# A new table of planned durations and a new table of priorities for the order of work on one core

## What is computed

```
x = x + 0.5 * moe0(norm(x))      # 24 experts, hidden 512, best 2 of 24 per token
x = x + linear_attention(norm(x))
x = x + 0.5 * moe0(norm(x))
x = x + 0.5 * moe1(norm(x))      # 8 experts, hidden 256, best 2 of 8, and a shared expert
x = x + causal_attention(norm(x))
x = x + 0.5 * moe1(norm(x))
```

## Time and profile before

| | us |
|---|---|
| median of 3 runs | 971.14 |
| lowest and highest | 970.65, 973.02 |
| the profiled execution's time | 970.65 |
| its span in the profile | 969.3 |

### The profile page before, as it was taken

One profiled execution on the slowest core, in us unless ns is written; L12 is line 12 of the kernel. 1 busy time (PEld: TensorE's weight loads), 2 busy tenths in 40 slices (PEclk: granted clock), 3 DMA queues, 4 the chain that ended last, 5 costly groups with the idle time before them and its releaser, 6 DMA issues. The chain is left out here.

```text
span 969.3 us, 25617 instructions
## 1 busy us (share of the span) xinstructions
PE 813.2 (84%) x9531; PEld 694.9 (72%) x9531; DVE 660.3 (68%) x2266; ACT 636.3 (66%) x1197; POOL 497.6 (51%) x519
## 2 busy tenths in 40 slices
PE   5898899998997477899999899874989998997940
PEld 3444899996886245798998789752777867786940
DVE  4798864477767897788467871479668979882122
ACT  4466788889895386688899775542748665773420
POOL 0076560065001777136366077777753575477775
PEclk9899999999999598799999999976999999998985
DMA  8789865473334323695657339842674374556852
GB/s 266 239 262 348 215 150 106 94 145 78 65 78 87 77 64 97 144 204 125 133 136 149 61 100 232 163 114 71 146 131 99 75 155 102 129 140 158 193 137 76
DMA packets 254167, 134.32 MB, mean 139 GB/s; under 512 B 171936, under 2 KB 232288, under 8 KB 254048
## 3 DMA queue, kind: packets, MB, share of 16 engines
q1 hardware_dynamic: 237664, 99.11, 44.5%
q0 software_dynamic: 16384, 33.59, 13.2%
HBM read 40.09 MB, written 56.89 MB: 100 GB/s over the span
## 5 line engine op out<-in xcount | busy, mean ns | idle before, releaser
L2540 POOL DMA_INDIRECT got<-y_l,slot_index x256 | 245.6, 960 | 249.0 <-DMA y_l<-y 83.4
L2520 POOL DMA_INDIRECT rows<-rows_sent,slot_index x192 | 189.3, 986 | 189.3 <-issue 93.9
L1711 PE MATMUL bank<-turned,first_high_l 128*128 128x128 f16 x1248 | 225.6, 221 | 23.1 <-DVE hid L2065 11.1
L1712 PE MATMUL bank<-turned,first_high_l 128*128 128x128 f16 x1248 | 225.3, 220 | 0.0
L1713 PE MATMUL bank<-turned,first_low_l 128*128 128x128 f16 x1248 | 225.2, 220 | 0.0
L2065 DVE SCALAR_TENSOR_TENSOR hid<-bank,hid 128x512 f16<-128x512 f32 x220 | 145.7, 686 | 84.2 <-ACT hid L1957 82.2
L1950 ACT ACTIVATE bank<-bank 128x512 f32<-128x512 f32 x220 | 128.4, 591 | 36.4 <-PE bank L1713 32.7
L2332 DVE SCALAR_TENSOR_TENSOR x_res<-got,share,x_res 128x128 f32<-128x128 f32 x256 | 77.6, 349 | 108.5 <-DMA got<-y_l,slot_index 106.2
L1711 PEld LDWEIGHTS bank<-turned,first_high_l 128*128 x1248 | 123.2, 99 | 30.6 <-issue 29.5
L1957 ACT ACTIVATE hid<-bank 128x512 f16<-128x512 f32 x220 | 129.0, 599 | 7.1 <-PE bank L1750 3.0
L1712 PEld LDWEIGHTS bank<-turned,first_high_l 128*128 x1248 | 123.1, 99 | 3.4 <-issue 1.9
(11 more groups left out here) (304 smaller groups left out, 1669.4 us busy)
## 6 DMA issues: line engine op xcount, KB each, us to landing
y_l<-y SPq DMA_DIRECT2D x92, 256.0 KB
rows<-own SPq DMA_DIRECT2D x14, 512.0 KB, 5.9
got<-in_w_dram SPq DMA_DIRECT2D x27, 256.0 KB, 4.5
hid<-in_w_dram SPq DMA_DIRECT2D x25, 256.0 KB, 3.6
got<-y_l,slot_index POOLq DMA_INDIRECT x256
rows<-rows_sent,slot_index POOLq DMA_INDIRECT x192, 2.4
y_l<-y SPq DMA_DIRECT2D x12, 192.0 KB
x_res<-in_x_dram SPq DMA_DIRECT2D x8, 256.0 KB, 4.5
```

The lines of the kernel that those rows point to most:

```text
L1711: t.do.matmul(out, cut_of(high[c], e), xh, start=True, stop=False)
L1712: t.do.matmul(out, cut_of(high[c], e), xl, start=False, stop=False)
L2520: d = g.do.indirect_dma_start(rows_dram[s], at, rows[:, 2 * D * i:2 * D * i + 2 * D], None)
L2540: d = g.do.indirect_dma_start(got_mem[slot][:, col:col + D], None, y_dram[layer][s][layer.team(ev.i)], at)
```

## The change

Two tables of the plan are replaced; no other line is touched. In `work`, the planned time of some steps becomes another one. The `EARLIER` table becomes another one as a whole: the entries for GpSimd (GP) and SyncE (SY) are gone, so that their steps go by 2p + s alone (unlisted expert steps on all engines but PE by -10 besides), and most entries of ScalarE (SC), TensorE (PE) and VectorE (VE) have other values.

```
-        "halve_0": [[(PE, 1.25, 0.2), (SC, 0.6, 0.1)]], "halve_1": [[(PE, 0.95, 0.2), (SC, 0.6, 0.1)]],
+        "halve_0": [[(PE, 1.1, 0.2), (SC, 0.6, 0.1)]], "halve_1": [[(PE, 0.95, 0.2), (SC, 0.6, 0.1)]],
-        "norm_a": [[(VE, 3.0, 0.1), (SC, 1.6, 0.15)]],
-        "norm_g": [[(VE, 3.0, 0.1), (SC, 1.6, 0.15)] if ev.p else [(VE, 1.15 if ev.i % 2 else 5.4, 0.1)]],
+        "norm_a": [[(VE, 2.73, 0.1), (SC, 1.6, 0.15)]],
+        "norm_g": [[(VE, 2.73, 0.1), (SC, 1.6, 0.15)] if ev.p else [(VE, 1.15 if ev.i % 2 else 5.4, 0.1)]],
-        "score": [[(PE, 0.5 if ev.p > 1 else 0.7 if ev.p else 0.95, 0.2), (VE, 0.2, 0.1)]],
-        "shared1": [[(PE, 1.6, 0.2), (SC, 1.2, 0.15)]], "shared2": [[(PE, 2.55, 0.2), (VE, 0.7, 0.1)]],
+        "score": [[(PE, 0.7 if ev.p else 0.95, 0.2), (VE, 0.2, 0.1)]],
+        "shared1": [[(PE, 1.4, 0.2), (SC, 1.3, 0.15)]], "shared2": [[(PE, 2.3, 0.2), (VE, 0.7, 0.1)]],
-        "scatter": [[(GP, 1.265 * TOP_K * tokens, 2.2)]], "gather": [[(GP, 1.23 * TOP_K * BT, 2.4)]], "add": [[(VE, 3.2, 0.1)]],
+        "scatter": [[(GP, 1.0 * TOP_K * tokens, 2.2)]], "gather": [[(GP, 1.0 * TOP_K * BT, 2.4)]], "add": [[(VE, 3.0, 0.1)]],
-        "la_qk": [[(PE, 2.3, 0.2), (SC, 1.45, 0.15)]], "la_vg": [[(PE, 1.85, 0.2), (SC, 1.3, 0.15)]],
-        "la_second": [[(PE, 2.65, 0.2), (VE, 1.4, 0.1)]], "la_soft": [[(SC, 3.7, 0.15), (VE, 1.4, 0.1)]],
-        "la_heads": [[(PE, 1.15, 0.2), (VE, 0.2, 0.1)]],
+        "la_qk": [[(PE, 1.9, 0.2), (SC, 1.3, 0.15)]], "la_vg": [[(PE, 1.85, 0.2), (SC, 1.3, 0.15)]],
+        "la_second": [[(PE, 2.8, 0.2), (VE, 1.4, 0.1)]], "la_soft": [[(SC, 3.9, 0.15), (VE, 1.4, 0.1)]],
+        "la_heads": [[(PE, 1.0, 0.2), (VE, 0.2, 0.1)]],
-        "la_out": [[(PE, 1.5, 0.2), (VE, 0.7, 0.1)]],
+        "la_out": [[(PE, 1.4, 0.2), (VE, 0.7, 0.1)]],
-        "ca_score": [[(PE, 2.4, 0.2), (VE, 3.0, 0.1), (SC, 3.3, 0.15)]], "ca_flip": [[(PE, 1.5, 0.2), (SC, 1.5, 0.15)], [(VE, 0.2, 0.1)]],
+        "ca_score": [[(PE, 2.4, 0.2), (VE, 3.0, 0.1), (SC, 3.3, 0.15)]], "ca_flip": [[(PE, 1.3, 0.2), (SC, 1.5, 0.15)], [(VE, 0.2, 0.1)]],
...
-EARLIER = {(GP, "gather"): -2, (GP, "gather", 2): -3, (GP, "scatter"): 3, (GP, "scatter", 0): 3, (GP, "scatter", 2): -4, (GP, "scatter", 3): 2,
...
- (SC, "ca_flip"): 0, (SC, "ca_score"): 3, (SC, "hid", 1): -3, (SC, "l1", 1): 0.5, (SC, "l1", 2): -1, (SC, "la_soft"): 3, (SC, "norm_a"): -3,
...
- (SY, "fetch"): -1, (SY, "fetch", 0): -4, (SY, "fetch", 1): 3, (SY, "fetch", 3): 2, (SY, "send_a"): -2, (SY, "send_g"): -1, (SY, "ystore"): -4,
...
- (PE, "ca_flip"): -4, (PE, "ca_score"): -2, (PE, "la_out"): -4, (PE, "la_second"): -2, (PE, "la_vg"): 2, (PE, "score", 2): -4,
...
- (VE, "add", 1): 0, (VE, "add", 2): 1, (VE, "add", 3): 3, (VE, "hid"): -2, (VE, "hid", 0): -3, (VE, "norm_g"): -4, (VE, "r_top"): -3, (VE, "r_norm"): -4,
...
+EARLIER = {(SC, "bias"): 0, (SC, "ca_flip"): -1, (SC, "ca_score"): -3, (SC, "hid", 0): 0, (SC, "hid", 1): -1, (SC, "l1"): -2, (SC, "l1", 1): 1, (SC, "la_soft"): -4, (SC, "norm_a"): -0.5,
...
+ (PE, "ca_flip"): -1, (PE, "ca_score"): 2, (PE, "la_out"): -2, (PE, "la_vg"): -0.5, (PE, "score", 2): 2,
...
+ (VE, "add"): 3, (VE, "add", 1): 2, (VE, "add", 2): 0.5, (VE, "hid"): 0, (VE, "hid", 0): -4, (VE, "hid", 1): -3, (VE, "norm_g"): -3, (VE, "r_top"): 1, (VE, "r_norm", 2): 3,
...
```

More of the change, by code:

```diff
@@ new lines @@
+EARLIER = {(SC, "bias"): 0, (SC, "ca_flip"): -1, (SC, "ca_score"): -3, (SC, "ca_v"): 3, (SC, "gates_1"): -1, (SC, "hid", 0): 0, (SC, "hid", 1): -1, (SC, "l1"): -2, (SC, "l1", 0): -1, (SC, "l1", 1): 1, (SC, "l1", 2): -1, (SC, "l1", 3): -3, (SC, "la_qk"): -3, (SC, "la_soft"): -4, (SC, "la_vg"): 3, (SC, "late_split"): -4, (SC, "norm_a"): -0.5, (SC, "norm_g", 1): 1, (SC, "norm_g", 2): 0.5, (SC, "norm_g", 3): -0.5, (SC, "r_gap"): -3, (SC, "r_gap", 1): -1, (SC, "r_soft"): 0.5, (SC, "r_soft", 2): 3, (SC, "r_soft", 3): -1, (SC, "send_a"): 2, (SC, "send_g", 1): -0.5, (SC, "send_g", 3): 2, (SC, "shared1"): -3, (SC, "shared1", 3): -0.5, (SC, "split_0"): -0.5, (SC, "split_1"): 0.5, (SC, "turn_a"): 0.5, (SC, "turn_g"): -4, (SC, "ystore"): -0.5, (SC, "ystore", 0): 1, (SC, "ystore", 2): 0.5, (PE, "ca_flip"): -1, (PE, "ca_out"): -1, (PE, "ca_q"): 0.5, (PE, "ca_score"): 2, (PE, "ca_v"): 1, (PE, "halve_0"): 2, (PE, "la_heads"): -2, (PE, "la_mix"): 0.5, (PE, "la_out"): -2, (PE, "la_qk"): -0.5, (PE, "la_vg"): -0.5, (PE, "r_end", 0): -3, (PE, "r_end", 1): -3, (PE, "r_rank"): 1, (PE, "r_rank", 0): -3, (PE, "r_rank", 1): -3, (PE, "r_rank", 2): 3, (PE, "r_rank", 3): 2, (PE, "score"): -0.5, (PE, "score", 1): 2, (PE, "score", 2): 2, (PE, "shared1"): 1, (PE, "shared2"): -4, (PE, "shared2", 3): -1, (PE, "split_0"): -3, (PE, "turn_a"): -3, (VE, "add"): 3, (VE, "add", 1): 2, (VE, "add", 2): 0.5, (VE, "bias"): 0, (VE, "ca_flip"): 0.5, (VE, "ca_k"): -3, (VE, "ca_out"): -3, (VE, "ca_score"): -3, (VE, "empties"): 2, (VE, "hid"): 0, (VE, "hid", 0): -4, (VE, "hid", 1): -3, (VE, "la_heads"): 0.5, (VE, "la_mix"): 1, (VE, "la_second"): 1, (VE, "la_soft"): -2, (VE, "norm_a", 1): -0.5, (VE, "norm_g"): -3, (VE, "norm_g", 0): 1, (VE, "norm_g", 3): -1, (VE, "r_end", 0): 3, (VE, "r_end", 2): -1, (VE, "r_end", 3): -4, (VE, "r_gap", 0): -2, (VE, "r_gap", 1): 1, (VE, "r_norm", 2): 3, (VE, "r_page", 1): 3, (VE, "r_rank"): -4, (VE, "r_rank", 0): -0.5, (VE, "r_rank", 2): -4, (VE, "r_rank", 3): 0.5, (VE, "r_send"): 3, (VE, "r_send", 1): -1, (VE, "r_share"): -1, (VE, "r_share", 1): -0.5, (VE, "r_share", 2): 3, (VE, "r_share", 3): 3, (VE, "r_slot"): -3, (VE, "r_slot", 0): 0, (VE, "r_slot", 1): 2, (VE, "r_slot", 2): 0.5, (VE, "r_soft", 3): -1, (VE, "r_top"): 1, (VE, "r_top", 0): 0.5, (VE, "r_top", 2): -1, (VE, "score"): 0.5, (VE, "score", 1): -0.5, (VE, "score", 2): 1, (VE, "score", 3): 3, (VE, "send_a"): 0, (VE, "send_g", 1): -1, (VE, "send_g", 3): 3, (VE, "shared2", 2): 2, (VE, "split_1"): -0.5}
```

1 line of the change is left out of this document (removed).

## The result

| | before, beside it | after |
|---|---|---|
| median | 972.08 us | 1012.35 us |
| lowest, highest | 970.65, 975.33 | 1011.15, 1014.36 |
| profiled execution, span | 970.65, 969.3 | 1013.01, 1011.7 |
| mean granted clock of PE | 0.927 | 0.913 |

After by before is 1.0411 [1.0379, 1.0444]: 40.3 us slower. The forecast was 988: right in direction, less than half the size, and the time lies just outside the range of 956 to 1012. (A slot is the time from the start of one indirect transfer to the start of the next.)

A forecast was written before the change was run, and what follows sets the result against it. The bound varied by stretch; from 489 us POOL set the end, with 405.5 us of fixed work plus 69.6 of gaps. Terms 10 + 2 + 5 = 17 on 970.65 gave 988 us, range 956 to 1012.

The forecast's parts named there:

- POOL's slot: POOL's transfers: the trace has 1.258 us each, the new table 1.0, putting the plan 8.3 us ahead after 32 transfers.
- Term (a): Layer-0 stretches, 196 to 236 and 494 to 534: late gathers hold DVE's adds, then PE; 5 us each, +10.
- Term (b): Stretch 311 to 352: chain already at POOL's and DVE's pace, so little extra waiting; +2 us, bounds 0 to 4.
- POOL's precedence itself changes little: Final gathers against last scatters on POOL: their swapped ranks were held to be worth nothing where POOL is the bound.
- Term (c): From 489 us: POOL's work fixed, only its 69.6 us of gaps can move; +5 us, bounds -28 to +35.
- Term (d): Stretches before 196 us: same table but for the split and the scatter; 0 us, bounds -3 to +3.
- The other durations: PE entries at full clock: new table nearer the trace by 0.15, 0.4 and 0.25 us, counted for the new version.
- Better line: Routed rounds: new priorities close POOL gaps of 19.4 and 8.5 us, giving 955 us; chance 0.22.
- Nothing moves: Whole kernel: stalls fall where POOL would be waited for anyway, its sum fixed; about 971 us, chance 0.08.
- Stalls feed on each other: DVE held by late adds, PE by DVE, POOL by its pace; 1017 us, chance 0.15.
- the first two signs of being wrong: Round 2's first gather at 489 us or earlier, or POOL's gaps from there under 55 us.
- the third: A gap in POOL's last 48 gathers would mean the tail's bound had changed to PE's experts.

The follow-up runs named there:

- item 3: Only POOL's planned slot changed: the kernel before with 1.0 us, 1054.2 us; the kernel after with 1.265 and 1.23 us, 1040.46 us.
- Item 6: The kernel after with stream 0's first scatters of round 1 planned behind stream 1's gathers of round 1; 1018.21 us, ratio 1.0468.
- Item 4: The kernel before with all new durations except POOL's slot, priorities old; 1011.32 us, ratio 1.0399.
- e6b: The kernel before with POOL transfers planned at 1.0 us instead of 1.265 and 1.23, all else old; 1054.2 us, ratio 1.0831.
- e7b: The kernel after with POOL's two entries set back to 1.265 and 1.23 us, all else new; 1040.46 us, ratio 1.0689.
- e9b: The kernel before with all new durations but POOL's, old priorities, run on the chip without the 17% slowdown; 1011.32 us, ratio 1.0399.
- other times new: The kernel before with all new durations but POOL's, old priorities; ratio 1.0387 on the slower chip, 1.0399 in the later run.

## Why the prediction came out too small

**POOL's slot** (1.258 us, table 1.0): right, and shown as the edit that makes the chip late (item 3 and the table above). It is 1.264 over the whole row after.

**Term (a), 5 us in each layer-0 stretch.** The place of the mechanism was wrong: DVE's waits for gathers went from 3.3 to 5.4 and from 4.5 to 3.0, and PE's idle time in the two stretches grew by 0.6 and 1.8 us only. Counted up to the last y, the first gave 3.2 us, most of it behind the gathers (PE is idle for 10.1 us from the first gather to the last y, for 6.9 before); the second gave 2.6 (round 2's first scatter is 17.9 us later after a start 15.3 later), which are part of the gaps of (c). Sum 5.8 for 10.

**Term (b), 2 us in 311 to 352, bounds 0 to 4.** Measured 12.1 up to the first gather of round 2 (15.3 - 3.2). The scatter alone made the gather 12.4 - 3.2 = 9.2 us later. The sentence that failed is "POOL's precedence itself changes little". I compared the ranks only for the final gathers. Stream 0's first round-1 scatter and stream 1's round-1 gathers changed places as well (ranks 2 + 3 = 5 and 3 - 2 = 1 before, 2 and 3 after), on the one queue that was about to be late. Item 6 adds that the place was not the cause: with it undone the time comes out no better.

**Term (c), 5 us of gaps from 489 on.** This is the step that failed by the most: the gaps grew by 28.1, inside the bounds of -28 and +35 and far from the value taken. I had written both causes down (a plan that takes PE for the bound spends nothing on feeding POOL; a late POOL meets work that is ready) and wrote "these two nearly cancel", with no row behind it. They don't. The new plan has POOL idle for 456.6 - 320 = 136.6 us of its row from 483.7 to 940.3, while the old one has 479.7 - 398.1 = 81.6. The chip needs 320 x 0.264 = 84.5 us more than planned and finds only 136.6 - 97.7 = 38.9 of that in the planned idle time; the other 45.6 are lateness: 20.6 when the row starts, 66.2 when it ends (1006.45, planned 940.3). Ready work meets a late POOL, then, for less than half of it. The runs give one reason: PE's strict list holds it at POOL's late rows (the three waits of 8.4, 13.3 and 4.9 us that its plan doesn't have), and so holds the next y that POOL waits for. How much of the 45.6 goes this way is not measured.

**Term (d), 0 before 196, bounds -3 to +3.** Stream 0's first gather starts 6.8 us earlier (189.48 for 196.24), which is outside the bounds. It is no gain: PE's idle time up to it is the same (23.6 and 23.7 us), and PE has only taken other work first.

**The other durations.** I took the better PE entries for a gain ("that counts for the new version"). Item 4 shows the opposite for a fixed table of priorities: 39 us lost, and the plan kept. How true the entries are and how well the priorities fit them are two things: the first shows in how late the chip is, the second in where the plan ends.

**The rivals.** "Better line" at 955: the plan did find one, 34 us shorter, and the chip could not run it. "Nothing moves" fell. "Stalls feed on each other" at 1017 came nearest, 5 us off, and was right in that POOL and PE hold each other up. Its route was partly wrong, so the nearness is partly luck: not through the adds (16.6 us priced, 5.8 came), and the pace is some 15 of the 40 us. Its price for (b) was 4 where 12 came, and for the gaps 26 where 28 came. Of the signs, the first gather of round 2 was to come at about 496 and came at 504, and the gaps were to be 70 to 80 and were 97.7; the first two signs of being wrong (489 or earlier, gaps under 55) looked for an error on the other side only, and the third, a gap within the last 48 gathers, didn't come.

**The bar and the slot.** The new entry of 1.0 is about the bar of the trace, and the bar is not the slot. A sentence of the Trainium skill (Perfetto Trace Analysis, "DMA Instruction — SWDGE (GPSIMD)") says that the profiler's end of such an instruction is where descriptors have been generated, and not where the data has moved. The trace after agrees: its last transfer has a bar of 0.94 us and lands 2.56 us after its start. The 0.30 us between one bar and the next transfer's start are a measurement of these traces; the page states no such interval.

Open: why the pace costs 18.7 us in the kernel after, 8 in e6b and 5 in the kernel before; how much of the fit's value lies in which priorities, since no run changed them one by one; and whether the new durations with POOL's true slot and priorities fitted to both would beat the kernel before, since no run has that.

## What to carry to other kernels

A planned duration is the time from one start to the next on its engine, not the bar of the profile: two POOL entries shortened by 0.23 and 0.265 us cost 81 us of 973 by themselves. Durations and priorities that fit each other are one piece: either half of this change alone was worse than the whole. Price such a change by playing both plans and asking how late the chip will be against each, above all on the queue that bounds the end. When a change makes a queue late, look at who consumes what it sends, at both kinds of its work, before you call the lateness covered.

## What the runs showed of the hardware

POOL's indirect transfer of 128 rows takes a slot of 1.26 us on average when nothing holds it, whatever the order: over the 320 transfers from round 2's first gather on it is 1.267 before, 1.264 after, 1.261 in e6b, 1.259 in e7b and 1.266 in e9b. Most bars are 0.94 to 1.0 us, with 0.30 behind each; single ones are longer, up to the 1.71 us at 304.95 in the kernel after.

On the chips on which the kernel before took 17% longer, POOL's instructions did not take longer. POOL's line for gathers in "other times new", on such a chip (e9) and then on one where the kernel before took 971.9 (e9b):

```profile
L2540 POOL DMA_INDIRECT got<-y_l,slot_index x256 | 245.7, 960 | 256.4 <-PE bank L1750 74.3 <-issue 60.1 <-remote 45.0
```

```profile
L2540 POOL DMA_INDIRECT got<-y_l,slot_index x256 | 246.2, 962 | 176.8 <-issue 69.2 <-PE bank L1750 64.3 <-PE bank L1572 25.1
```

The mean bar is 960 and 962 ns. On POOL, DVE and ACT the extra 160 us of the span are idle time (DVE is busy 663.1 and 661.8 us, ACT 633.0 and 634.0); PE is busy 879.7 for 819.5, at a mean granted clock of 0.885 for 0.918. Before POOL's gathers 45.0 us of the idle time end with a release that the trace can't place ("remote"). What caused it no run shows.
